# Both ends of a mixture-of-experts stage: where two engines' loops begin, extra identity transposes, and the first gathers' indices

## The chip, the cores and the metric

One core of a Trainium2 chip runs the whole program. The metric is device time in microseconds (us), the median of several executions. A profiled execution of its own gives the trace; its own time stands beside the span in the table below.

## What is computed

Input x has 8 sequences of 256 tokens with 512 features (2048 tokens, 16 tiles of 128), and a context of the same shape. The first half of the layer is grouped cross attention (32 query heads, 8 key and value heads). The second half, which the change touches, is a mixture of 32 experts with top 4 routing, each expert made of a large part (inner size 192) and a small shared part (inner size 128):

```python
x = x + xattn(layernorm(x), ctx, ctx, Wq, Wk, Wv, Wfc, bfc)
h = layernorm(x)
logits = h @ gate_w.T
rw = softmax(logits); _, sel = top_k(sigmoid(logits), 4)
w = take(rw, sel); w = w / w.sum(-1)
large = sum over e of (silu(h @ Wg[e]) * (h @ Wu[e]) * cw[e]) @ Wd[e]
small = the same with cWg, cWu, cWd, two experts sharing one chunk
x = x + large + 0.05 * small
```

All matrices are float32.

## The kernel before

There are three stages, each a block of its own with a program for every engine; all engines meet between two blocks.

**attention** (to about 396 us) computes the attention and stores the new x to `out` and its normalised rows to the table `xd` in device memory. ScalarE loads one set of function tables at its start (line 401) and uses the logarithm and the exponential there.

**route** (396 to 448 us) transposes the 16 tiles, computes the logits and the top 4, and sorts the (token, expert) pairs into slots of 128 rows, each slot of one expert. `transpose(t)` on TensorE (L1217) fills two PSUM buffers in turn; ScalarE's `x_evac(t)` (L1133) empties them, and transpose(t) waits for the evacuation of tile t - 2. ScalarE's program begins with `preload_act_table_set` (L1171), then two x_evac, then a logarithm and an exponential for the late tiles. Its results for the next stage are tables: `tok` (which rows of xd a slot gathers), `dst` (where its results are added), `slot_e`, `slot_buf`, and `turns` (how many loop turns there are). This input fills 78 slots. The weights of the first experts are loaded meanwhile.

**experts** (448 us to the end) runs the slots, two per loop turn; p is the slot's parity and selects one of two buffers. The loops are written for 48 turns with an `If(i < n)`, n = 39 here; the first turn (slots 0 and 1) stands ahead of the loop, and turns beyond n pass empty. For slot s:

- GpSimd `gather(s, p)`: waits until xg is free (turned and wt_ready of slot s - 2), copies column s of tok to gidx (L1501), waits for the copy, and gathers 128 rows of xd to xg with an indirect DMA (L1504).
- VectorE `turn(s, p)` (L1599): a 32 x 32 block transpose of xg into xb. `weights_of(s, p)` (L1590, L1592): the routing weights of the slot's expert. ScalarE `x_move(s, p)` (L1545): four transfers xb to xT, which finish the transpose.
- TensorE `gate_up(s)` (L1636): 8 matmuls for gates, 8 for ups. ScalarE `silu` (L1550). VectorE `gated(s)` (L1603, L1605): the product in `a`.
- TensorE `transpose_a(s)` (L1645): 3 transposes to at_ps, in the program of the next slot, ahead of its gate_up. VectorE `at_evac(s)` (L1582) copies them to aT. TensorE `down(s)` (L1653): 6 matmuls to y_ps, behind the next slot's gate_up.
- ScalarE `y_evac(s)` (L1556): y_ps to yb; it waits until the add of slot s - 2 has landed. GpSimd `add(s, p)`: copies column s of dst to yidx (L1510), waits for yb and until all earlier adds have landed (`y_added`), and adds yb to rows of `out` with an indirect DMA (L1518).

Each engine's order is written out by hand. VectorE's loop turn is at_evac(s - 1), turn(s + 2), gated(s), weights_of(s + 2), once for each parity; its last at_evac stands behind the loop. GpSimd's is add(s - 1), gather(s + 4), with the last add behind the loop. ScalarE's is silu(s), x_move(s + 2), y_evac(s - 1). TensorE's is transpose_a(s - 1), gate_up(s), down(s - 1), with transpose_a and down of the last slot behind the loop. Three weight buffers hold the experts; SyncE loads the next expert as slots finish.

Of the kernel before, what the change touches and what calls it, by code (L numbers as in the profile page):

```python
# [6 lines left out]
ACT = mybir.ActivationFunctionType  # L7
AX = mybir.AxisListType
F32 = mybir.dt.float32
# [5 lines left out]
P = 128  # L15
D = 512
# [950 lines left out]
IW = IL + IS  # L967
# [23 lines left out]
def route(nc, gw, gw_loaded, xs, ident, new, xd, out, tabs, wts, W, w_loaded, kept, xd_stored):  # L991
# [4 lines left out]
    tok, dst, slot_e, slot_buf, cum_i, turns = tabs  # L996
    with ExitStack() as ctx:  # L997
# [130 lines left out]
        def _(act):  # L1128
# [42 lines left out]
            act.preload_act_table_set("natural_log_exp_and_others")  # L1171
# [258 lines left out]
def experts(nc, ident, xd, out, tabs, wts, W, w_loaded):  # L1430
# [4 lines left out]
    with ExitStack() as ctx:  # L1435
# [10 lines left out]
        sg = [sb(f"sg{i}", [P, IW], F32) for i in range(2)]  # L1446
# [6 lines left out]
        at_ps, y_ps = ps("at_ps", [P, 4, P]), ps("y_ps", [P, D])  # L1453
# [41 lines left out]
        def _(pool):  # L1495
            def gather(s, p):

                if not (isinstance(s, int) and s < 2):
                    pool.wait_ge(turned, s - 1)
                    pool.wait_ge(wt_ready, s - 1)  # L1500
                pool.tensor_copy(idx[p][:, :], tok[:, bass.ds(s, 1)]).then_inc(idx_ready, 1)  # L1501
                pool.wait_ge(idx_ready, s + 1)
                pool.sem_inc(passed, 1)
                pool.indirect_dma_start(xg[p][:, :], None, xd[:, :], bass.IndirectOffsetOnAxis(idx[p][:, :], 0))\  # L1504
                    .then_inc(x_loaded[p], DMA)
# [17 lines left out]
            gather(4, 0)  # L1523
            add(0, 0)
            gather(5, 1)
            n, last = count(pool)
            with pool.Fori(1, NS // 2) as i:
                with pool.If(i < n):
                    for p in range(2):
                        add(i * 2 + p - 1, 1 - p)  # L1530
                        gather(i * 2 + p + 4, p)
# [6 lines left out]
        def _(act):  # L1538
# [24 lines left out]

            x_move(0, 0)
# [14 lines left out]
        def _(dve):  # L1579
# [40 lines left out]
            n, last = count(dve)  # L1620
            with dve.Fori(1, NS // 2) as i:  # L1621
                with dve.If(i < n):  # L1622
                    for p in range(2):
                        at_evac(i * 2 + p - 1, 1 - p)
                        turn(i * 2 + p + 2, p)
                        gated(i * 2 + p, p)
                        weights_of(i * 2 + p + 2, p)
            at_evac(last + 1, 1)

        @block.tensor  # L1630
        def _(pe):
            def gate_up(s, p, buf):
# [34 lines left out]

            slot(0, 0, first=True)
# [6 lines left out]
            transpose_a(last + 1, 1)  # L1675
            down(last + 1, 1, pe.value_load(slot_buf[0:1, bass.ds(last + 1, 1)], min_val=0, max_val=NW - 1))
# [63 lines left out]
```

## Time and profile before

| | |
|---|---|
| time, median of 3 runs | 1054.81 us (1053.97 to 1056.63) |
| profiled execution, its own time | 1054.6 us |
| its span, first to last instruction | 1052.9 us |
| mean granted TensorE clock (1.0 is 2.4 GHz, 0.5 is 1.2 GHz) | 0.968 |
| TensorE busy | 983.6 us, 93% |
| VectorE, ScalarE, GpSimd busy | 524.5, 314.0, 300.2 us |
| device memory | 101.29 MB read, 29.36 MB written |

Times within an execution count from the start of its span. PE is TensorE's matmuls, PEld its weight loads, DVE is VectorE, ACT ScalarE, POOL GpSimd, SP SyncE; a name with q, such as ACTq, is the engine's sequencer, which issues instructions and DMAs. A wait is put down to what released it; "issue" is time in which the engine waited for nothing that the profile shows. The profile shows the granted clock of TensorE for each stretch.

### The profile page before, as it was taken

The page shows a single profiled execution, that of the slowest core. Times are in us where ns is not written, and L with a number is a line of the kernel's source. Part 1 is how long each engine was busy: PE and PEld are TensorE (multiplying, and loading weights), DVE is VectorE, ACT ScalarE, POOL GpSimd, SP SyncE. Part 2 cuts the span into 40 slices and gives each one's busy share as a digit, 9 for nine tenths or more (in the row PEclk, how much of TensorE's full clock was granted, in tenths as well). Part 3 has the DMA queues.
Part 4 walks back from the last instruction along what each step waited for, and adds up shares of the span by engine and source line. Part 5 has one row for each costly group of instructions (what it writes and reads, how often), then busy time and mean ns, then how long its engine had stood idle before and what let it go on. Part 6 is the DMA issues. An engine that isn't in the chain of part 4 may idle for free.

```text
span 1052.9 us, 18703 instructions
## 1 busy us (share of the span) xinstructions
PE 983.6 (93%) x5163; PEld 723.9 (69%) x5164; DVE 524.5 (50%) x1233; ACT 314.0 (30%) x631; POOL 300.2 (29%) x399
## 2 busy tenths in 40 slices
PE   8789999999999987449999999999999999999994
PEld 6556667676665545337787777878777787877872
DVE  5677677777677727923333333333333333333331
ACT  2245465555555536801111111111111111111110
POOL 3012101011120002223443434344343443434432
PEclk9999999999999999569999999999999999999997
DMA  6153234331431019138888998989888899889563
GB/s 215 44 163 77 75 84 102 87 87 58 121 80 51 32 41 354 47 83 201 217 219 199 253 252 213 259 206 256 201 224 213 207 259 244 214 207 252 113 112 71
DMA packets 102603, 168.23 MB, mean 160 GB/s; under 512 B 15520, under 2 KB 65824, under 8 KB 98208
## 3 DMA queue, kind: packets, MB, share of 16 engines
q1 hardware_dynamic: 36624, 103.11, 31.3%
q0 software_dynamic: 17792, 43.30, 22.6%
q10 hardware_dynamic: 48144, 21.25, 7.3%
q8 instruction: 27, 0.44, 0.2%
q14 instruction: 16, 0.13, 0.0%
HBM read 101.29 MB, written 29.36 MB: 124 GB/s over the span
## 4 chain that ended last, share of the span: by engine, by line
PE 55%; DMA 1%; issue 1%; DVEq 0%; DVE 0%; ACTq 0%; POOL 0%; ACT 0%; POOLq 0%
PE y_ps L1653 19%; PE g_ps L1636 17%; PE u_ps L1636 16%; PE at_ps L1645 2%; DMA xg<-xd,gidx 0%; DMA xT<-xb 0%; ACTq L1545 0%; POOL out_x L1518 0%; DVEq L1621 0%; DVE xb L1599 0%; ACT sg L1550 0%; DVEq L1586 0%; ACT yb L1556 0%; DVE aT L1582 0%; DVEq L1622 0%
## 5 line engine op out<-in xcount | busy, mean ns | idle before, releaser
L1653 PE MATMUL y_ps<-W,aT 128*128 x468 | 216.2, 598 | 3.6 <-DVE aT L1582 3.6
L1518 POOL DMA_INDIRECT out_x<-yb,yidx x78 | 125.3, 1606 | 278.4 <-ACT yb L1556 159.7
L1636 PE MATMUL g_ps<-W,xT 128*128 x624 | 192.5, 452 | 12.8 <-DMA xT<-xb 12.8
L519 DVE TENSOR_REDUCE mx<-s 128x2 f32<-128x512 f32 x256 | 163.6, 682 | 59.4 <-PE s L710 58.6
L398 ACT ACTIVATE pt<-stp 128x512 f32<-128x512 f32 x256 | 139.1, 596 | 146.6 <-PE stp L724 145.9
L1636 PE MATMUL u_ps<-W,xT 128*128 x624 | 180.7, 432 | 0.0
L1636 PEld LDWEIGHTS g_ps<-W,xT 128*128 128x128 f32 x624 | 168.3, 311 | 15.2 <-issue 15.1
L1636 PEld LDWEIGHTS u_ps<-W,xT 128*128 128x128 f32 x624 | 171.0, 308 | 0.1
L1653 PEld LDWEIGHTS y_ps<-W,aT 128*128 128x128 f32 x468 | 89.6, 192 | 85.7 <-issue 79.6
L1599 DVE STREAM_TRANSPOSE xb<-xg 128x512 f32<-128x512 f32 x80 | 89.1, 1114 | 102.6 <-DMA xg<-xd,gidx 99.8
L1550 ACT ACTIVATE sg<-g_ps 128x320 f32<-128x320 f32 x78 | 34.2, 438 | 302.4 <-PE u_ps L1636 302.4
L1603 DVE SCALAR_TENSOR_TENSOR a<-u_ps,wt,sg 128x192 f32<-128x192 f32 x78 | 32.6, 418 | 160.8 <-ACT sg L1550 158.9
L1556 ACT COPY yb<-y_ps 128x512 f32<-128x512 f32 x78 | 45.7, 585 | 201.2 <-DMA out_x<-yb,yidx 125.4
L1504 POOL DMA_INDIRECT xg<-xd,gidx x82 | 82.7, 1008 | 65.4 <-POOL gidx L1501 64.7
L710 PE MATMUL s<-kst,qst 96*128 96x256 bf16 x512 | 81.6, 274 | 10.8 <-DVE mx L519 9.9
L1582 DVE COPY aT<-at_ps 128x384 f32<-128x384 f32 x78 | 43.5, 558 | 86.8 <-PE at_ps L1645 81.9
L724 PE MATMUL stp<-qst,kst 98*128 98x256 bf16 x512 | 78.5, 276 | 4.2 <-DMA qst<-nm 4.1
L710 PEld LDWEIGHTS s<-kst,qst 96*128 96x128 bf16 x512 | 43.7, 97 | 51.8 <-DVE mx L519 24.5
L740 PE MATMUL ov<-pt,vx 128*32 128x256 f32 x1024 | 70.3, 393 | 2.0 <-ACT xo L382 2.0
L1501 POOL COPY gidx<-tok 128x1 uint32 (+1 forms) x82 | 60.0, 732 | 28.1 <-POOLq L997 17.2
L724 PEld LDWEIGHTS stp<-qst,kst 98*128 98x128 bf16 x512 | 49.4, 98 | 17.7 <-issue 5.7
L1645 PEld LDWEIGHTS at_ps<-ident,a 128*128 128x128 f32 x234 | 30.2, 140 | 43.7 <-issue 42.0
(203 smaller groups left out, 869.5 us busy)
## 6 DMA issues: line engine op xcount, KB each, us to landing
W<-in_wts SPq DMA_DIRECT2D x32, 1280.0 KB
W<-in_wts SPq DMA_DIRECT2D x32, 768.0 KB
xT<-xb ACTq DMA_DIRECT2D x320, 64.0 KB
qst<-q SPq DMA_DIRECT2D x42, 256.0 KB, 5.0
xs<-in_x SPq DMA_DIRECT2D x8, 512.0 KB, 3.7
ctxT<-in_ctx SPq DMA_DIRECT2D x8, 512.0 KB, 4.2
out_x<-xs SPq DMA_DIRECT2D x16, 256.0 KB, 2.3
kst<-k SPq DMA_DIRECT2D x48, 64.0 KB, 2.3
```

Of the source, the lines that this page charges most:

```text
L398: act.activation(pt[g % 2][:, 2 * (j % 2) + r, :, :], stp[n % STP][:, :, :], ACT.Exp, scale=DH ** -0.5).then_inc(exp_done, 1)
L519: dve.tensor_reduce(mx[j // CH % 2][:, h:2 * G:G], s1[r][:, :, :], AX.X, ALU.max)\
L710: m = pe.matmul(s1[r][:, t, :], qst[b % 2][0:ROWS_QK, head(j, r), t * P:(t + 1) * P], kst[b % 2][0:ROWS_QK, head(j, r) // C, :], start=Tru ...
L724: m = pe.matmul(stp[n % STP][:, t, :], kst[b % 2][0:ROWS_ST, head(j, r) // C, t * P:(t + 1) * P], qst[b % 2][0:ROWS_ST, head(j, r), :], st ...
L740: m = pe.matmul(ov[c * VW:(c + 1) * VW, g % 2, :], vx[b % 2][:, t, g % 2 * C + c, :], pt[(b * G + g) % 2][:, c, t, :], start=(t == 0), sto ...
L1501: pool.tensor_copy(idx[p][:, :], tok[:, bass.ds(s, 1)]).then_inc(idx_ready, 1)
L1504: pool.indirect_dma_start(xg[p][:, :], None, xd[:, :], bass.IndirectOffsetOnAxis(idx[p][:, :], 0))\
L1518: pool.indirect_dma_start(out[:, :], bass.IndirectOffsetOnAxis(yidx[p][:, :], 0), yb[p][:, :], None, compute_op=ALU.add).then_inc(y_added, ...
L1599: dve.transpose(xb[p][:, :].rearrange("p (j r c) -> p j c r", r=Q, c=C), xg[p][:, 0:D]).then_inc(turned, 1)
L1636: m = pe.matmul(ps_[p][:, 0:IW], xT[p][:, :, c], W[:, bass.ds(buf, 1), (2 * c + g) * IW:(2 * c + g + 1) * IW] .rearrange("p a f -> p (a f) ...
L1645: m = pe.transpose(at_ps[:, c, :], a[p][:, c * P:(c + 1) * P], ident[:, :])
L1653: m = pe.matmul(y_ps[:, :], aT[p][:, c, :], W[:, bass.ds(buf, 1), GW + c * D:GW + (c + 1) * D].rearrange("p a d -> p (a d)"), start=(c == ...
```

## The change

In `route`, the explicit table load at the head of ScalarE's program goes. In `experts`:

- ScalarE begins with a Silu of one column of the identity, whose result nobody reads. It brings the table load of Silu to the start of its program.
- GpSimd's first four gathers take their indices from `tok` itself, with no copy and no wait for it; the others copy as before. gather(5) moves ahead of add(0), and the loop turn becomes gather(s + 4), add(s - 1).
- VectorE's at_evac(1) moves ahead of the loop, and a loop turn becomes turn(s + 2), gated(s), weights_of(s + 2), at_evac(s), for each parity. Nothing stands behind the loop.
- TensorE transposes the identity 32 times into a PSUM buffer of its own ahead of slot 0, and 5 times between the last transpose_a and the last down.

```diff
--- before.py
+++ after.py
@@ -1168,7 +1168,6 @@
                     act.activation(rown[:, t, :, :], away[t % 2][:, :, :], ACT.Relu, bias=number[:, t:t + 1],
                                    scale=minus[:, t:t + 1]).then_inc(rown_ready, 1)
 
-            act.preload_act_table_set("natural_log_exp_and_others")
             x_evac(0)
             x_evac(1)
             act.wait_ge(var_ready, 1)
@@ -1443,14 +1442,14 @@
         wt = [sb(f"wt{i}", [P, 2], F32) for i in range(2)]
         xb = [sb(f"xb{i}", [P, D], F32) for i in range(2)]
         xT = [sb(f"xT{i}", [P, P, C], F32) for i in range(2)]
-        sg = [sb(f"sg{i}", [P, IW], F32) for i in range(2)]
+        sg, first = [sb(f"sg{i}", [P, IW], F32) for i in range(2)], sb("e_first", [P, 1], F32)
         a = [sb(f"a{i}", [P, IP], F32) for i in range(2)]
         aT = [sb(f"aT{i}", [P, 3, P], F32) for i in range(2)]
         yb = [sb(f"yb{i}", [P, D], F32) for i in range(2)]
 
         g_ps = [ps(f"g_ps{i}", [P, 512]) for i in range(2)]
         u_ps = [ps(f"u_ps{i}", [P, 512]) for i in range(2)]
-        at_ps, y_ps = ps("at_ps", [P, 4, P]), ps("y_ps", [P, D])
+        at_ps, y_ps, idle_ps = ps("at_ps", [P, 4, P]), ps("y_ps", [P, D]), ps("idle_ps", [P, P])
 
         experts_ready, slots_done = sem("experts_ready"), sem("slots_done")
         idx_ready, x_loaded = sem("idx_ready"), [sem(f"xg_loaded{i}") for i in range(2)]
@@ -1498,10 +1497,14 @@
                 if not (isinstance(s, int) and s < 2):
                     pool.wait_ge(turned, s - 1)
                     pool.wait_ge(wt_ready, s - 1)
-                pool.tensor_copy(idx[p][:, :], tok[:, bass.ds(s, 1)]).then_inc(idx_ready, 1)
-                pool.wait_ge(idx_ready, s + 1)
-                pool.sem_inc(passed, 1)
-                pool.indirect_dma_start(xg[p][:, :], None, xd[:, :], bass.IndirectOffsetOnAxis(idx[p][:, :], 0))\
+                if isinstance(s, int) and s < 4:
+                    rows = tok[:, s:s + 1]
+                else:
+                    pool.tensor_copy(idx[p][:, :], tok[:, bass.ds(s, 1)]).then_inc(idx_ready, 1)
+                    pool.wait_ge(idx_ready, s - 3)
+                    pool.sem_inc(passed, 1)
+                    rows = idx[p][:, :]
+                pool.indirect_dma_start(xg[p][:, :], None, xd[:, :], bass.IndirectOffsetOnAxis(rows, 0))\
                     .then_inc(x_loaded[p], DMA)
 
             def add(s, p):
@@ -1521,14 +1524,14 @@
             for s in range(4):
                 gather(s, s % 2)
             gather(4, 0)
+            gather(5, 1)
             add(0, 0)
-            gather(5, 1)
             n, last = count(pool)
             with pool.Fori(1, NS // 2) as i:
                 with pool.If(i < n):
                     for p in range(2):
+                        gather(i * 2 + p + 4, p)
                         add(i * 2 + p - 1, 1 - p)
-                        gather(i * 2 + p + 4, p)
             add(last + 1, 1)
             pool.wait_ge(y_added, last * DMA + 2 * DMA)
             for p in range(2):
@@ -1561,6 +1564,7 @@
                 if not first:
                     y_evac(s - 1, 1 - p)
 
+            act.activation(first[:, :], ident[:, 0:1], ACT.Silu).then_inc(passed, 1)
             x_move(0, 0)
             x_move(1, 1)
             slot(0, 0, first=True)
@@ -1617,18 +1621,23 @@
             turn(3, 1)
             gated(1, 1)
             weights_of(3, 1)
-            n, last = count(dve)
+            at_evac(1, 1)
+            n, _ = count(dve)
             with dve.Fori(1, NS // 2) as i:
                 with dve.If(i < n):
                     for p in range(2):
-                        at_evac(i * 2 + p - 1, 1 - p)
                         turn(i * 2 + p + 2, p)
                         gated(i * 2 + p, p)
                         weights_of(i * 2 + p + 2, p)
-            at_evac(last + 1, 1)
+                        at_evac(i * 2 + p, p)
 
         @block.tensor
         def _(pe):
+            def keep_clock(n):
+
+                for _ in range(n):
+                    pe.transpose(idle_ps[:, :], ident[:, :], ident[:, :])
+
             def gate_up(s, p, buf):
                 pe.wait_ge(x_ready[p], moved(s, p))
                 for ps_, g in ((g_ps, 0), (u_ps, 1)):
@@ -1665,6 +1674,7 @@
                 if not first:
                     down(s - 1, 1 - p, pe.value_load(slot_buf[0:1, bass.ds(s - 1, 1)], min_val=0, max_val=NW - 1))
 
+            keep_clock(32)
             slot(0, 0, first=True)
             slot(1, 1)
             n, last = count(pe)
@@ -1673,6 +1683,7 @@
                     slot(i * 2, 0)
                     slot(i * 2 + 1, 1)
             transpose_a(last + 1, 1)
+            keep_clock(5)
             down(last + 1, 1, pe.value_load(slot_buf[0:1, bass.ds(last + 1, 1)], min_val=0, max_val=NW - 1))
 
 
```

## Rows read from the trace of the kernel before

**Rows 1.** The page: busy us (share of span) xinstructions of each engine

```profile
PE 983.6 (93%) x5163; PEld 723.9 (69%) x5164; DVE 524.5 (50%) x1233; ACT 314.0 (30%) x631; POOL 300.2 (29%) x399
```

**Rows 2.** Busy time by stretch: stretch, length, engines' busy, granted clock, DMA share, GB/s

```profile
480.00:1000.00 520.00, 519.95 (x1771) 408.21 (x1770) 188.58 (x426) 72.34 (x142) 212.76 (x284) 1.00 0.88 222
```

**Rows 3.** Timeline, routing stage's start: start, us, engine, what [idle before <- releaser]

```profile
396.26 1.28 ACT L1171 ACT_TABLE_LOAD   x1 [8.01 <-PEq L50]
...
396.30 1.06 PE L1217 MATMUL r_xt<-ident,xs 128*128 128x128 f32 x8 [1.85 <-PEq L50]
...
397.56 1.07 ACT L1133 COPY r_xnT<-r_xt 128x512 f32<-128x512 f32 x2
...
398.20 3.56 PE L1217 MATMUL r_xt<-ident,xs 128*128 128x128 f32 x16 [0.83 <-ACT r_xnT L1133]
```

**Rows 4.** Busy time by stretch, around three changes of the granted clock

```profile
398.00:399.00 1.00, 0.80 (x5) 0.77 (x6) 0.00 (x0) 0.97 (x4) 0.42 (x4) 0.76 0.77 236
463.00:464.00 1.00, 1.00 (x4) 0.86 (x3) 0.00 (x0) 0.00 (x0) 0.00 (x0) 0.81 0.00 0
1038.00:1040.00 2.00, 1.60 (x2) 0.84 (x3) 0.25 (x1) 0.00 (x0) 0.63 (x1) 0.50 0.70 135
```

**Rows 5.** Chain that ended last, expert stage's start: start, us, what

```profile
448.68 0.19 POOL gidx L1501
...
448.91 0.85 issue
449.77 3.58 DMA xg<-xd,gidx
...
459.66 4.25 PE g_ps L1636 x8
```

**Rows 6.** Timeline, the last 25 us

```profile
1030.44 2.74 PE L1653 MATMUL y_ps<-W,aT 128*128 x6
...
1032.47 0.15 DVE L1590 COPY wt<-xg 128x1 f32 x1 [0.68 <-DVE a L1605]
...
1033.43 0.58 ACT L1556 COPY yb<-y_ps 128x512 f32<-128x512 f32 x1 [2.36 <-DMA out_x<-yb,yidx]
...
1034.26 0.54 PE L1645 MATMUL at_ps<-ident,a 128*128 128x128 f32 x3 [1.08 <-issue]
1035.02 1.61 POOL L1518 DMA_INDIRECT out_x<-yb,yidx  x1 [2.60 <-ACT yb L1556]
...
1037.62 1.01 POOL L1504 DMA_INDIRECT xg<-xd,gidx  x1 [0.80 <-POOL gidx L1501]
1037.69 0.56 DVE L1582 COPY aT<-at_ps 128x384 f32<-128x384 f32 x1 [4.88 <-issue]
...
1038.40 5.43 PE L1653 MATMUL y_ps<-W,aT 128*128 x6 [3.60 <-DVE aT L1582]
...
1041.67 0.18 POOL L1510 COPY yidx<-dst 128x1 uint32 x1 [3.05 <-issue]
...
1043.95 0.58 ACT L1556 COPY yb<-y_ps 128x512 f32<-128x512 f32 x1 [9.93 <-PE y_ps L1653]
1045.54 1.61 POOL L1518 DMA_INDIRECT out_x<-yb,yidx  x1 [3.68 <-ACT yb L1556]
```

**Rows 7.** Timeline, expert stage's start: a gather and ScalarE's table load

```profile
457.66 0.98 POOL L1504 DMA_INDIRECT xg<-xd,gidx  x1 [0.79 <-issue]
...
459.79 1.28 ACT L1550 ACT_TABLE_LOAD   x1 [15.41 <-issue]
```

**Rows 8.** Tile out_x, adds' start to landing: first 480 to 1030 us, then from 1000

```profile
DMA to landing us min/median/max: 4.7/5.1/8.1
...
DMA to landing us min/median/max: 4.4/4.8/5.0
```

**Rows 9.** Chain that ended last, the eight up matmuls of a middle slot

```profile
484.81 2.15 PE u_ps L1636 x8
```

**Rows 10.** Timeline of GpSimd: an add that waited for the one before, and the next

```profile
632.61 1.60 POOL L1518 DMA_INDIRECT out_x<-yb,yidx  x1 [5.11 <-DMA out_x<-yb,yidx]
638.40 1.61 POOL L1518 DMA_INDIRECT out_x<-yb,yidx  x1 [1.99 <-ACT yb L1556]
```

## The prediction

> **What bounds the kernel now.** I read the page first, then the busy time by stretch, then the chain of waits at both ends of the expert stage, then the timeline there. The page has TensorE busy for 93% of the span [rows 1]. In the middle of the expert stage, from 480 to 1000 us, TensorE is busy 519.95 of 520 us at the full granted clock, while VectorE needs 188.58 us and GpSimd 212.76 us [rows 2]. Nothing in this stretch gives time back unless TensorE's own work shrinks, and the change leaves that work alone. A gain can only come from where TensorE waits: the start of the routing stage, the 13 us between the routing stage and the first expert matmul, and the last 20 us. I cost the change place by place, against the profiled execution's 1054.6 us (its span is 1052.9 us), which lies 0.2 us under the median of 1054.81 us.
>
> **Part 1, the table load in the routing stage.** ScalarE begins the stage with a load of 1.28 us at 396.26, and its first copy of a transposed tile follows at 397.56 [rows 3]. TensorE has begun its first eight transposes at 396.30; the first four, which the copy needs, take about half of their 1.06 us plus the tail of one, so they end near 396.93. TensorE resumes only at 398.20, after that copy [rows 3]. Without the load the copy starts near 396.96: 397.56 - 396.96 = 0.6 us earlier. The stage up to its tables is a chain of TensorE, ScalarE and VectorE with no outside date in it that I found, so 0.6 us carries through. Bounds: 0 (if the function tables must be loaded before the logarithm after all, see the rivals) and 1.28 + 0.3 us (if the earlier transposes also keep the clock up; it falls at 398 to 399 after 1.1 us of transposes and a gap [rows 4]). I take 0.6, since the row shows which transposes the copy must still await. The Trainium skill ("ScalarE: Activation LUTs", What ACT_TABLE_LOAD costs) adds a drain of about 1.38 us to the 1.28 us of a load, and by it the removal could be worth up to 2 us; here the copy follows 0.02 us after the load, so the trace does not agree.
>
> **Part 2, the first gathers.** The chain runs index copy 448.68 (0.19 us), 0.85 us without any wait, gather 449.77, which lands 3.58 us later; then the transpose, four transfers to xT, and the first expert matmul at 459.66 [rows 5]. The copy and its semaphore go: 0.19 + about 0.1 us. Whether the 0.85 us goes too depends on whose it is. In the last 20 us the same 0.80 us stands ahead of a gather at 1037.62, and 1.01 us stands between the end of yb at 1044.53 and the last add at 1045.54, where no copy lies in between [rows 6]. So a DMA_INDIRECT starts 0.8 us after its release whatever released it, and I let the 0.85 us stay: gain 0.3 us, bounds 0.2 and 1.1. The Trainium skill ("DMA: Bandwidth & Descriptors", Latency and other measured facts) gives about 1 us as the first-byte latency of a DMA issued by GpSimd, which speaks for the gap being the DMA's own and against this edit. Against the gain: gather 1 can follow gather 0 at once instead of waiting a second for its own copy, and gather 3 comes 1.2 us before its 457.66 [rows 7], so its data moves beside the first xT transfers. An add lands 4.4 to 5.0 us after its start in the last 50 us and 5.1 in the middle, with weight loads beside it [rows 8], so company costs some 0.5 to 1 us; only a part of it can meet xT(0). I take -0.15, which leaves 0.15 us; with both ends -0.6 to +1.1.
>
> **Part 3, the table load of Silu** moves from 459.79 to the stage's start. Both places are hidden: it ends at 461.07 [rows 7] while the activation waits until 466.1 for the matmuls, and at the start ScalarE waits until 454.49 for the first transpose. Nothing, unless the start shrinks by 4 us.
>
> **Part 4, 32 transposes before slot 0.** TensorE is free from 447 to 459.66. Sixteen transposes take 3.56 us at a mostly low clock, small gaps included [rows 3], 0.22 us each, so 32 take about 7.1 us from 448.7 and end by 455.8, or by 457.4 at 0.27 us each, before the first matmul near 459.4: no delay. Do they help? The first slot's 16 matmuls take 459.66 to 466.08, 6.42 us, and the clock rises inside, in 463 to 464 [rows 4]; at the full clock eight of them take 2.15 us [rows 9], sixteen 4.3 to 4.4, so 2.0 us is there to win. But once the clock has risen the rest of the 32 goes by fast, and TensorE idles for 2 to 5 us before slot 0. At the routing stage's start it had 1.85 us idle, 1.1 us of transposes, a gap, and fell to half [rows 4]. I take 0 for the forecast, bounds -0.6 (the clock rises later relative to an earlier start) and +2.0. The Trainium skill ("TensorE: Matmul & The Clock Gate", What's actually happening) says the window is free-running and does not reset with the kernel, so the point of the rise differs between runs; no row of one execution can show that.
>
> **Part 5, the loops in the middle.** VectorE's cyclic order (at_evac, turn, gated, weights_of) is unchanged. GpSimd's becomes gather(s+4) before add(s-1). The gather waits for weights_of, which ends 2 us after slot s's up matmuls (the last one at 1032.62); the add waits for yb, which ends 1.4 us later (1034.01) [rows 6]. So the gather runs first without holding the add for long: copy 0.2, gap 0.8, gather 1.0, copy 0.2, gap 0.85, so the add starts about 0.7 us later in each slot than now. ScalarE needs that add landed two slots (14.66 us) later. An add lands 5.1 us after its start, 8.1 at worst [rows 8], so 3 us of slack stay: nothing.
>
> **Part 6, the end.** Step by step from [rows 6]:
> - VectorE now finishes weights_of at 1032.81, then passes nine empty turns of its loop (39 of 48 are used) and reaches the last at_evac only at 1037.69, though the transposes were done at 1034.80. Inside the loop at_evac starts at 1034.85, ends 1035.41, and TensorE starts down 0.14 us later, at 1035.55 instead of 1038.40: 2.85 us.
> - The five transposes begin at 1034.80 and take 5 x 0.11 to 0.16 us at the full clock (three take 0.54 with their tail), so they end at about 1035.5: free. Down now runs at half clock, 5.43 us [rows 4, 6], where the slot before took 2.74 us. The stretch 1038 to 1040 is at half, behind an idle from 1034.80 to 1038.40, so with TensorE busy I expect 2.74: another 2.7 us. Down ends near 1038.3 instead of 1043.83.
> - ScalarE's last yb comes after its own empty turns. It dispatches the yb before at 1033.43; nine turns at VectorE's 0.53 us give 1038.2, a tie. It ends at 1038.95 instead of 1044.53, 5.6 us earlier.
> - GpSimd is late next. gather(81) now comes first: released at 1032.62, started near 1033.65, over at 1034.66; copy, gap, and add(76) starts at 1035.7 instead of 1035.02. Its empty turns end near 1039.7 (now the gather at 1037.62 is dispatched 0.7 us earlier, and the next copy is at 1041.67: 4.7 us). But the last add must await the landing of add(76), and this add now has a gather 2 us ahead of it. A landing takes 4.4 to 5.0 us in the last 50 us [rows 8]; with company up to 1 us more. I take 5.5: landed at 1041.2, plus 0.8, last add at 1042.0 instead of 1045.54. Gain 3.5 us; bounds 2.9 (landing 6.1) and 5.6 (landing hidden, the ScalarE date). What follows the last add is unchanged.
>
> **Sum.** 0.6 + 0.15 + 3.5 = 4.25 us off 1054.6: 1050.35, and with the 0.2 us to the median 1050.5 us. Its own range, with landing and gather bounds: 1049.2 to 1051.9.
>
> **Rivals.**
> - The clock survives into slot 0. For: there are 32 transposes, and a run of them keeps TensorE busier than anything since 420 us. Against: the idle behind them. It gives 2.0 us more: 1048.5.
> - The last add is not held by the landing of the one before, so the whole 5.6 us comes through. For: an early landing, of 4.4, and a GpSimd order that yields faster than I reckon. Against: five adds in a row at 4.8 to 5.0. It gives 2.1 us more: 1048.4.
> - The change does not do what it says in the routing stage: with no explicit load, one is put before the logarithm anyway. Nothing is saved, or one more load of 1.28 us is paid between logarithm and exponential. With the first gathers disturbing xT as well (-0.6), the sum is 0 - 0.6 + 3.5 = 2.9 or less: 1051.9. Against: the attention stage uses logarithm and exponential with a single load, and the trace shows no load between.
> - Slower: adds queue behind gathers. Each add awaits the one before, so adds are spaced at least landing + 0.8 us; a slot is 7.33 us, and it decides from a mean landing of 6.5 us. The median is 5.1, and a gather 2 us ahead may add up to 1 us and more under the weight loads (8.1 is in the record [rows 8]). At 7.0 the surplus is 0.47 us in each of 76 slots, 36 us less the 5 us that the double buffers hold: 1054.8 - 4 + 31 = 1082. Adds that await the one before sit idle for up to 5.11 us where the usual is 3.5, and the next is back in step [rows 10], which speaks against.
>
> **Chances.** Forecast 0.52, clock in slot 0 0.17, landing hidden 0.10, load put back or start disturbed 0.15, slower 0.06. A measurement of this kernel tells 0.3%, 3.2 us, from no change: faster means under 1051.65. The first three cases lie there but for 0.04 of the forecast's own: 0.75. Same: 0.15 + 0.04 = 0.19. Slower: 0.06. The range holds 8 in 10 from 1047.9 (part of both faster rivals) to 1052.3.
>
> **What would show it.** Right: no ScalarE load in the routing stage and its first copy about 0.7 us after its start; the first GpSimd gather 0.8 us after the stage opens; the first expert matmul still in a stretch of half clock; at_evac within 0.1 us of the last transposes; down in 2.7 us; the last add released by the landing of the add before it. Wrong: a stretch inside 480 to 1000 us with TensorE idle, a landing over 6.5 us in the middle, or the last add released by yb.

## The result and the profile after

The changed kernel took 1047.54 us (median of 5, 1046.58 to 1049.79) against 1054.2 us for the kernel before in the same comparison: a ratio of 0.9938, 95% interval 0.9915 to 0.996. Two later comparisons, each on one chip, gave 0.9948 (0.993 to 0.9967) and 0.9949 (0.9926 to 0.9972). So it saves 5.4 to 6.7 us, 0.5 to 0.6%. The forecast was 1050.5 us, a saving of 4.3, and its range began at 1047.9: the sign was right, the size too small. The measured median lies 0.4 us below the range; the medians of the two later comparisons, 1048.3 and 1048.23 us, lie inside it, so that it lies outside at all is partly chance.

The profiled execution took 1049.79 us, its span 1048.1. The page of the changed kernel has TensorE with more work, the 37 added transposes, in a shorter span (busy us, share of the span, instructions), and TensorE's wait for xT, ahead of its gates, at 4.4 us where 12.8 stood, since the transposes fill the rest (group of instructions: busy us, mean ns, idle before and its releaser):

```profile
PE 988.3 (94%) x5200; PEld 730.1 (70%) x5201; DVE 522.7 (50%) x1233; ACT 312.6 (30%) x631; POOL 297.8 (28%) x395
...
L1645 PE MATMUL g_ps<-W,xT 128*128 x624 | 192.4, 451 | 4.4 <-DMA xT<-xb 4.4
```

I cut both profiled executions at the same events, read from the timelines, in us:

| stretch | before | after | difference | forecast |
|---|---|---|---|---|
| attention: span's start to the first transpose of the routing stage | 396.30 | 397.52 | +1.22 | 0 |
| routing stage, to its last table | 51.84 | 50.12 | -1.72 | -0.6 |
| last table to gather 0 | 1.63 | 1.30 | -0.33 | -0.3 |
| gather 0 to the first expert matmul | 9.89 | 10.22 | +0.33 | +0.15 |
| slot 0: first matmul to its silu | 6.44 | 7.17 | +0.73 | 0 |
| silu to the first transposes of a | 1.20 | 1.21 | +0.01 | 0 |
| slots: first to last transposes of a | 566.96 | 565.75 | -1.21 | 0 |
| end: last transposes of a to the span's end | 18.64 | 14.81 | -3.83 | -3.5 |
| span | 1052.9 | 1048.1 | -4.8 | -4.25 |

The pair differs by 4.8 us, the medians by 6.7. The attention stage, whose code is the same, ends between 394.01 and 399.10 us in the sixteen executions profiled for this study, so a single time carries up to 5 us that no edit made. From here on I compare stretches.

**Routing stage.** Timeline of the changed kernel, against [rows 3]. The load is gone and nothing took its place. The copy starts 0.66 us behind the first transpose instead of 1.26, TensorE idles 0.24 instead of 0.83 us, and its next transposes come at full speed:

```profile
397.52 1.06 PE L1216 MATMUL r_xt<-ident,xs 128*128 128x128 f32 x8 [1.85 <-PEq L50]
...
398.18 1.07 ACT L1133 COPY r_xnT<-r_xt 128x512 f32<-128x512 f32 x2 [8.71 <-PE r_xt L1216]
...
398.82 1.15 PE L1216 MATMUL r_xt<-ident,xs 128*128 128x128 f32 x8 [0.24 <-ACT r_xnT L1133]
```

**Start of the expert stage.** Chain that ended last (start, us, what), against [rows 5]. The 0.19 us of the index copy are gone and the wait without a name stays: 0.90 us, where 0.85 stood:

```profile
448.04 0.90 issue
448.94 3.57 DMA xg<-xd,tok
```

**First slot.** Timeline and busy time by stretch. The 32 transposes take 6.57 us; the clock rises near their end, at 454.1, and falls again at 457.5, 1.6 us before the first matmul. It is back in 464 to 465 only, later into the slot than in [rows 4]:

```profile
448.19 6.57 PE L1639 MATMUL idle_ps<-ident 128*128 128x128 f32 x32 [1.80 <-PEq L997]
...
459.16 4.65 PE L1645 MATMUL g_ps<-W,xT 128*128 x8 [4.40 <-DMA xT<-xb]
```

```profile
457.00:458.00 1.00, 0.00 (x0) 0.00 (x0) 0.00 (x0) 0.00 (x0) 0.00 (x0) 0.77 0.73 261
464.00:465.00 1.00, 1.00 (x4) 0.81 (x3) 0.00 (x0) 0.00 (x0) 0.00 (x0) 0.82 0.00 0
480.00:1000.00 520.00, 520.00 (x1775) 409.38 (x1774) 185.74 (x426) 72.58 (x142) 212.02 (x284) 1.00 0.85 223
```

**The end.** Timeline, against [rows 6]. VectorE's copy comes 0.04 us behind the transposes' end, down starts at 1034.59 and takes 2.84 us instead of 5.43:

```profile
1033.29 0.54 PE L1654 MATMUL at_ps<-ident,a 128*128 128x128 f32 x3 [1.10 <-issue]
...
1033.67 0.71 PE L1639 MATMUL idle_ps<-ident 128*128 128x128 f32 x5
1033.87 0.56 DVE L1586 COPY aT<-at_ps 128x384 f32<-128x384 f32 x1 [2.50 <-PE at_ps L1654]
1034.59 2.84 PE L1662 MATMUL y_ps<-W,aT 128*128 x6 [0.20 <-DVE aT L1586]
1034.75 1.60 POOL L1521 DMA_INDIRECT out_x<-yb,yidx  x1 [1.14 <-DMA out_x<-yb,yidx]
1037.54 0.59 ACT L1559 COPY yb<-y_ps 128x512 f32<-128x512 f32 x1 [4.48 <-PE y_ps L1662]
...
1040.35 1.59 POOL L1521 DMA_INDIRECT out_x<-yb,yidx  x1 [1.37 <-DMA out_x<-yb,yidx]
```

The chain of its last 20 us shows what is late next. Two adds wait one for the other, and each landing (4.88 and 4.76 us) stands in the chain:

```profile
1029.04 4.88 DMA out_x<-yb,yidx
...
1034.75 4.76 DMA out_x<-yb,yidx
...
1040.35 1.59 POOL out_x L1521
```

The last yb is ready at 1038.13; the last add waits until 1039.51 for the landing and starts 0.84 us later.

### The profile page after: what moved, and what is told of

It is laid out like the page before. It is cut to its first block, busy times and chain, and to the rows that moved or that the text cites. A ratio compares the mean times of both kernels' runs of the same rounds, so it can differ in the third digit from the quotient of the medians.

```text
span 1048.1 us, 18692 instructions
## 1 busy us (share of the span) xinstructions
PE 988.3 (94%) x5200; PEld 730.1 (70%) x5201; DVE 522.7 (50%) x1233; ACT 312.6 (30%) x631; POOL 297.8 (28%) x395
## 4 chain that ended last, share of the span: by engine, by line
PE 54%; DMA 2%; issue 1%; POOL 0%; DVE 0%; ACTq 0%; ACT 0%; DVEq 0%; POOLq 0%
PE y_ps L1662 18%; PE g_ps L1645 17%; PE u_ps L1645 16%; PE at_ps L1654 2%; DMA out_x<-yb,yidx 1%; DMA xg<-xd,tok 0%; DMA xT<-xb 0%; ACTq L1548 0%; POOL out_x L1521 0%; DVE xb L1603 0%; POOL xg L1507 0%; ACT sg L1553 0%; DVEq L1590 0%; DVE a L1607 0%; DVE a L1609 0%
## 5 line engine op out<-in xcount | busy, mean ns | idle before, releaser
L1662 PE MATMUL y_ps<-W,aT 128*128 x468 | 213.7, 592 | 0.2 <-DVE aT L1586 0.2
L1507 POOL DMA_INDIRECT xg<-xd,gidx x78 | 78.5, 1007 | 64.4 <-POOL gidx L1503 62.2
L1503 POOL COPY gidx<-tok 128x1 uint32 (+1 forms) x78 | 14.3, 183 | 196.4 <-DVE wt L1594 196.4
```

The lines of the kernel that those rows point to most:

```text
L1662: m = pe.matmul(y_ps[:, :], aT[p][:, c, :], W[:, bass.ds(buf, 1), GW + c * D:GW + (c + 1) * D].rearrange("p a d -> p (a d)"), start=(c == ...
```

## The experiments

My theory was that the terms of the sum are the right ones and that the surplus over the forecast is the clock's, which rises and falls at other places in each execution. The rival was that the changed kernel differs in something fixed, such as the middle of the stage, to which the forecast gave nothing. Kernels are named by their labels. All stretches of all traces stand in one table behind the runs.

**The changed kernel once more, `after_again`.** 

> The changed kernel once more, for a second trace. My theory: of the 6.7 us between the medians, 4.8 us stand in the profiled pair, and the rest is where TensorE's clock rises and falls, which differs between executions; so this trace shows the clock changes of routing stage and first slot at other places, a routing stage of 50 to 52.5 us and a first slot of 4.5 to 7.2 us, and the same last 15 us within 0.3 us. Rival: the changed kernel differs from the old one in something fixed that the first pair hid (then routing stage and first slot are as in the first trace within 0.2 us). Both: ratio near 0.994, 1047 to 1049 us.

1048.3 us, ratio 0.9948. Routing stage 50.12, slots 565.77, end 14.89 us: each within 0.1 us of the first trace. The gather to the first matmul took 11.28 instead of 10.22 us. So the shorter routing stage and the shorter middle are fixed, and the rival is right on these two, where the theory failed; the start of the stage is what varies.

**VectorE's part alone, `at_evac_in_loop`.** The kernel before with

```diff
             weights_of(3, 1)
+            at_evac(1, 1)
...
-                        at_evac(i * 2 + p - 1, 1 - p)
                         turn(i * 2 + p + 2, p)
                         gated(i * 2 + p, p)
                         weights_of(i * 2 + p + 2, p)
-            at_evac(last + 1, 1)
+                        at_evac(i * 2 + p, p)
```

> The kernel before with VectorE's part alone: at_evac at the end of the loop turn. My theory: the last at_evac follows the last transposes within 0.1 us and down starts 2.9 us earlier, but GpSimd's old order now ends last: its index copy for the last add comes only after gather 81 and nine empty loop turns, at about 18.6 - 11.2 = 7.4 us behind the last transposes as before, so the last add starts 8.2 to 8.4 us behind them instead of 11.28: 3.0 us less. Without the five transposes down takes between 2.7 and 4.5 us, which is hidden. Median 3 us below before. Rival (the landing of the add before is what holds the last add): it starts 35.02 + 4.9 + 0.8 - 34.26 = 6.5 us behind the transposes, 4.8 us less.

Ratio 0.9988 (0.9972 to 1.0004). Its timeline:

```profile
1034.14 0.54 PE L1645 MATMUL at_ps<-ident,a 128*128 128x128 f32 x3 [1.12 <-issue]
1034.72 0.56 DVE L1582 COPY aT<-at_ps 128x384 f32<-128x384 f32 x1 [2.08 <-PE at_ps L1645]
1034.89 1.61 POOL L1518 DMA_INDIRECT out_x<-yb,yidx  x1 [2.63 <-ACT yb L1556]
1035.44 2.84 PE L1653 MATMUL y_ps<-W,aT 128*128 x6 [0.75 <-DVE aT L1582]
```

at_evac follows at once, down takes 2.84 us without any added transposes, and the last add starts 8.69 us behind the last transposes instead of 11.28: close to the 8.2 to 8.4 of GpSimd's old order and its empty turns, far from the 6.5 of the landing. The end is 16.26 instead of 18.64 us. By the ratio that makes 1.3 us in all, where 3 were expected. But the slots took 568.35 us, 1.4 us more than in the kernel before, and TensorE was busy for only 518.48 us of the 520 in the middle. The waits of TensorE in that stretch (us in total, times, longest) name the transfers to xT, which the prediction had left out:

```profile
PE g_ps L1636 <- DMA xT<-xb: 1.4, 2, 1.2
```

**GpSimd's part alone, `gather_first`.** The kernel before with

```diff
-            add(0, 0)
             gather(5, 1)
+            add(0, 0)
...
-                        add(i * 2 + p - 1, 1 - p)
                         gather(i * 2 + p + 4, p)
+                        add(i * 2 + p - 1, 1 - p)
```

> The kernel before with GpSimd's part alone: gather 5 ahead of add 0, and gather ahead of add in the loop turn. My theory as predicted: nothing in the middle, nothing at the end (the last add still waits for yb), 0 us. Rival, from the comparison of the two traces: before has six slots that are 0.2 to 0.3 us longer than 7.33 us, the changed kernel none, and this order removes them: the time from the first transposes of a to the last is 565.7 us instead of 567.0, 1.2 us less.

Ratio 0.9977 (0.9959 to 0.9996), 2.4 us less. The slots took 565.75 us, as in the changed kernel: the rival is right and the forecast's "nothing" wrong. Its routing stage, with the load in place, took 50.70 us; the clock did not fall in it.

**The load of the routing stage alone, `after_no_preload_only`.** The kernel before without the line `act.preload_act_table_set(...)` in `route`. 

> The kernel before without the explicit table load in the routing stage, nothing else. My theory: no other load takes its place; ScalarE's first copy starts 0.66 us after the first transpose instead of 1.26; TensorE's idle behind its first eight transposes falls from 0.83 to 0.24 us, and with it the clock stays at full through the first 5 us; the stage, from first transpose to the tables, takes 50.1 us instead of 51.84 (clock fell) or 50.70 (it did not). Rival (the shorter stage of the changed kernel was only the clock's chance): 51.2 us, 0.6 less than 51.84, with the clock down at 398 to 402. Medians: 1 to 1.7 us below before, or 0.6.

The routing stage took 50.10 us, the clock stayed at full, and no other load appeared. The ratio was 1.0008 (0.9988 to 1.0027): an edit that shortens its stage by 0.6 to 1.7 us in the traces can't be seen in the time at all, so this one is shown by the trace only.

**Small gathers, `before_small_gathers`.** The kernel before, with

```diff
-                pool.indirect_dma_start(xg[p][:, :], None, xd[:, :], bass.IndirectOffsetOnAxis(idx[p][:, :], 0))\
+                n, rows = (XW, xd[:, :]) if isinstance(s, int) else (68, xd.rearrange("n (k w) -> (n k) w", w=68))
+                pool.indirect_dma_start(xg[p][:, 0:n], None, rows, bass.IndirectOffsetOnAxis(idx[p][:, :], 0))\
```

> The kernel before, with its order on GpSimd, but each gather from slot 6 on brings only 68 columns instead of 544 (as many rows and descriptors, an eighth of the bytes; the rest of its tile keeps old values, so this leaves the experts' inputs out). My theory: the long slots in the middle (2 to 6 per execution, 1.1 to 2.6 us together) are slots in which the transfers to xT run beside the gather, which the old order starts 0.5 us ahead of them, and beside a weight load, and land late; with small gathers no slot is long, and first to last transposes take 565.77 us as with the new order. Rival (the new order helps by starting adds or gathers earlier, not by moving the gather's bytes away from xT's): 566.9 to 568.4 us as before.

The slots took 565.74 us with GpSimd's old order, and of the distances between the transposes of one slot and the next none was long but those that all these kernels have, the first (7.41 us) and the last (8.58 us, with the empty turns in it). So it is the gathers' bytes. Ratio 0.9987 (0.9973 to 1.0001): the time does not tell it from the kernel before, the stretches do. The timelines of one slot show where they were: in the kernel before the gather starts 0.5 us ahead of the four transfers to xT, and its data move beside them,

```profile
1015.61 1.01 POOL L1504 DMA_INDIRECT xg<-xd,gidx  x1 [0.80 <-POOL gidx L1501]
...
1016.11 2.52 ACTq L1545 DMA_DIRECT2D xT<-xb  x4
```

and in the changed kernel it starts 3.2 us behind them:

```profile
1015.13 2.60 ACTq L1548 DMA_DIRECT2D xT<-xb  x4
...
1018.34 1.01 POOL L1507 DMA_INDIRECT xg<-xd,gidx  x1 [0.80 <-POOL gidx L1503]
```

Sometimes xT then comes too late for the next slot. All seventeen long slots in the four traces with the old order and full gathers follow 7.0 to 7.1 us behind the issue of a weight load; but so do some 190 of the 283 slots there that are not long. That a weight load is needed is therefore likely, and what else picks the late ones is not shown. This is the longest case, in the chain of at_evac_in_loop, a slot of 8.81 us (the weight load began at 884.67):

```profile
884.49 8.63 DMA xT<-xb
893.12 0.24 issue
893.36 2.54 PE g_ps L1636 x8
```

**No empty turns, `before_39_turns`.** The kernel before with `Fori(1, 39)` for `Fori(1, NS // 2)` in the four loops. 

> The kernel before with the four loops written for 39 turns, as many as this input needs, instead of 48, so no empty turn is passed (the output is right for this input alone). My theory: the nine empty turns are what held the last at_evac (3.43 us behind the last transposes), delayed the last transposes on TensorE (1.08 us idle before them) and GpSimd's last copy. Here at_evac follows within 0.6 us of the transposes' start with VectorE's old order, the slot before them is 1.1 us shorter, down takes 2.7 to 2.8 us, and from the last transposes to the end 13.8 to 14.5 us pass instead of 17.5 to 18.6: together 4.5 to 5.5 us. Rival (at_evac was late for another reason on VectorE, such as the wait for its own weights_of): it stays 3 us behind.

1047.41 us, ratio 0.9933 (0.9911 to 0.9956): as much as the whole change. Its first to last transposes take 565.36 us: the last slot is 7.3 us long instead of 8.6, and three slots with late xT remain. The timeline has at_evac at once and no 1.1 us of idle before the last transposes:

```profile
1031.21 0.49 PE L1645 MATMUL at_ps<-ident,a 128*128 128x128 f32 x3
...
1031.74 0.56 DVE L1582 COPY aT<-at_ps 128x384 f32<-128x384 f32 x1 [0.73 <-PE at_ps L1645]
1032.50 2.84 PE L1653 MATMUL y_ps<-W,aT 128*128 x6 [0.81 <-DVE aT L1582]
```

The end took 15.29 us, more than the 13.8 to 14.5 expected: here too the last add waits for the landing of the one before, which starts 2.03 us behind the last transposes.

**Without the five transposes, `after_no_5`.** 

> The changed kernel without the five transposes between the last transpose_a and the last down. My theory: they are free and they give nothing either. Down starts 1.30 us behind the last transposes with or without them, since VectorE's copy ends then; without them down takes 2.84 us, or up to 4.5 if the clock falls; the last add waits for the landing of the add before it, at 7.1 to 7.3 us behind the last transposes, where yb is ready at 4.84; so the end stays at 14.8 to 14.9 us unless down takes more than 5.2 us. Rival (they hold the clock for down, and down decides): the end is 1.6 to 2.7 us later.

Down takes 2.84 us and starts 1.29 us behind the last transposes, the end 14.91 us, median 1048.32; ratio 0.996 (0.9943 to 0.9976). The five do nothing.

```profile
1032.47 0.56 DVE L1586 COPY aT<-at_ps 128x384 f32<-128x384 f32 x1 [2.51 <-PE at_ps L1654]
1033.18 2.84 PE L1662 MATMUL y_ps<-W,aT 128*128 x6 [0.75 <-DVE aT L1586]
```

**Without the 32, `after_no_32`.** 

> The changed kernel without the 32 transposes ahead of slot 0. My theory: they neither help nor harm, since TensorE idles 2.5 to 7 us behind them and the clock falls before or early in slot 0: slot 0 takes 6.3 to 7.5 us with or without, the gather to the first matmul 10.2 to 11.3 us as with them (its cost is the gathers'). Median within 1 us of the changed kernel, 1047.5 to 1048.5. Rival (the transposes' reads disturb the transfers): the gather to matmul time falls to 9.9 us with them gone.

Slot 0 took 7.22 us, the gather to the first matmul 10.14. The median was 1049.77 us (8 runs, 1045.13 to 1051.48), above the 1047.5 to 1048.5 expected, but the ratio, 0.9944 (0.9924 to 0.9963), is that of the changed kernel. The 32 do nothing either.

**72 of them, `after_72`.** 

> The changed kernel with 72 transposes before slot 0 instead of 32, so that TensorE is busy from the stage's opening to near the first expert matmul. My theory: 32 end at 454.8 and the clock falls again at 457.5, before slot 0, so they give nothing; 72 (about 27 at half clock, 0.2 us each, then 45 at 0.11 us: 10.3 us) end at about 458.5, the clock stays up, and slot 0's 16 matmuls take 4.4 to 4.7 us instead of 6.4 to 7.2: 2 to 2.7 us below the changed kernel. If the clock rises late they run on to at most 460, 1 us past the start of slot 0. Rival (transposes of the identity hold no clock through slot 0, or delay it): 0 or 1 us more than the changed kernel.

They took 9.6 us instead of 10.3, since the clock rose after 3 us, and ended 2.45 us before the first matmul. It fell again at 458.4, 1.4 us into slot 0, which took 6.42 us. The expectation failed; its number of transposes was too small. 1046.5 us, ratio 0.993 (0.9911 to 0.9949): 1.8 us under after_again on the same chip, which the stretches behind the attention stage do not explain (their sum is 0.4 us smaller), so nothing shows it to be a gain of the 72.

**Copies for gathers 1 to 3, `after_copies_1_to_3`.** The changed kernel with

```diff
-                if isinstance(s, int) and s < 4:
+                if isinstance(s, int) and s < 1:
...
-                    pool.wait_ge(idx_ready, s - 3)
+                    pool.wait_ge(idx_ready, s)
```

> The changed kernel, but only gather 0 takes its indices from tok; gathers 1 to 3 copy them first, as before. My theory: the time from gather 0's start to the first expert matmul was 9.89, 9.89 and 9.95 us in three kernels whose gathers 1 to 3 copy, and 10.22, 11.28 and 11.29 us in three whose gathers don't, so the earlier gathers run beside the transfers to xT(0) and cost 0.3 to 1.4 us, more than the 0.33 us that the missing copy of gather 0 gives. Here that time is 9.9 us, and the opening of the stage to gather 0 stays at 1.30 us from the tables: about 0.3 to 1.4 us less than the changed kernel up to slot 0. Rival (the longer time is something else, such as the 32 transposes or the early table load of Silu beside the transfers): it stays at 10.2 to 11.3 us.

10.05 us from the gather to the first matmul where 9.9 were expected, against 10.13 to 11.29 with the direct gathers in six traces. The median, 1048.37, does not show it.

**96 transposes and two gathers fewer, `best_96_skip`.** 

> The changed kernel with three edits: 96 transposes ahead of slot 0 instead of 32, only gather 0 straight from tok, and the last two gathers, whose rows no slot uses, left out. My theory: with 72 transposes TensorE was still idle for 2.45 us before slot 0 and the clock fell 1.7 us into it; 24 more at 0.11 us fill this, so slot 0 takes 4.5 us instead of 6.4 to 7.2 (unless the clock rises late: then they run up to 2 us into slot 0). Gather 0 to the first matmul 9.9 us instead of 10.2 to 11.3. At the end the add before the last starts 0.75 us behind the last transposes instead of 1.5, with no gather beside it, and lands after 4.4 us instead of 4.8: last add at 5.9 to 6.2 us instead of 7.1 to 7.3. Together 2 + 0.8 + 1.1 = 3.9 us below the changed kernel, near 1044 us. Rival (the end is held by GpSimd's nine empty turns and its index copy): last add at 6.8 us or later; and if the transposes delay slot 0, 1 us more there.

The transposes took 12.48 us and ran 1.4 us past the arrival of xT (VectorE's third block transpose, which waits for the same transfers, started at 457.09, the first matmul at 458.59). Slot 0 took 4.72 us. From gather 0 to the silu of slot 0 16.33 us passed, against 17.39 to 18.11 in the changed kernel, 16.33 in after_copies_1_to_3 and 14.98 and 15.09 with 80 transposes (below), so the delay took much of the gain back. At the end the add before the last started 1.62 us behind the last transposes although no gather stood ahead of it, 1.9 us after its yb was ready at 1030.01; I don't know why it took this long. The median, 1048.89 us, is no better than the changed kernel's, where 1044 was expected.

**80 transposes and the copies, `after_80_copies`.** The changed kernel with the edit of after_copies_1_to_3 and `keep_clock(80)`. 

> The changed kernel with 80 transposes instead of 32 and copies for gathers 1 to 3. 96 overran the arrival of xT by 1.4 us at an early rise of the clock (12.5 us in all), 72 ended 2.45 us short at 9.6. My theory: 80 take 10.5 us, up to 11.7 where the clock rises late, and xT arrives about 11.2 us after TensorE's start, so the clock stays up and slot 0 takes 4.5 to 4.7 us, at a gather to matmul of 9.9 to 10.4: 2 to 2.5 us less than the changed kernel up to the first transposes of a. Median 1046 to 1046.5. Rival (free-running changes of the clock take it away in part of the executions, and the overrun in others, so on the median nothing is left): 1048.

Timeline: 80 take 10.26 us, TensorE idles 0.75 us, the clock stays at full, and the eight gates take 2.54 us instead of 4.65:

```profile
447.57 10.26 PE L1639 MATMUL idle_ps<-ident 128*128 128x128 f32 x80 [1.80 <-PEq L997]
...
458.58 2.54 PE L1645 MATMUL g_ps<-W,xT 128*128 x8 [0.75 <-DMA xT<-xb]
```

Slot 0 took 4.73 us. 1047.04 us, ratio 0.9928 (0.9907 to 0.9949), where 1046 to 1046.5 was expected.

**The two side by side, `after_third` and `after_80_third`.** 

> The changed kernel, beside after_80_third on one chip. My theory: routing stage 50.1 us, slots 565.77 us, last 14.6 to 14.9 us as in both traces before; gather to first matmul 10.2 to 11.3, slot 0 6.3 to 7.5, attention anywhere from 394 to 399 us. 1047.5 to 1048.5 us.

> The kernel with 80 transposes and copies for gathers 1 to 3, beside the changed kernel on one chip. My theory: slot 0 at 4.7 us, the gather to the first matmul 9.9 to 10.3 us, everything else equal, so 2.3 us below after_third on the median, and spread as wide, since the spread is the attention stage's. Rival: the difference is lost where the clock rises late, and the two medians are within 1 us.

On one chip 1048.23 us (11 runs, 1046.11 to 1053.7; ratio 0.9949) and 1045.2 us (6 runs, 1044.14 to 1048.06; ratio 0.9924, 0.9894 to 0.9955): 3.0 us less. The intervals of the two ratios overlap, so the traces carry this more than the times: 4.73 us for slot 0 in both traces of the kernel with 80, 6.8 to 7.7 us in the three of the changed kernel. This is the lowest ratio of the study, though its interval overlaps with several others.

All stretches, in us:

| kernel | routing | gather 0 to matmul | slot 0 | slots | end |
|---|---|---|---|---|---|
| before | 51.84 | 9.89 | 6.44 | 566.96 | 18.64 |
| at_evac_in_loop | 51.85 | 9.89 | 6.37 | 568.35 | 16.26 |
| gather_first | 50.70 | 9.95 | 7.49 | 565.75 | 17.93 |
| after_no_preload_only | 50.10 | 9.95 | 7.40 | 566.89 | 17.47 |
| before_39_turns | 50.71 | 9.96 | 7.45 | 565.36 | 15.29 |
| before_small_gathers | 50.73 | 9.89 | 7.41 | 565.74 | 18.19 |
| changed kernel, three traces | 50.12, 50.12, 50.10 | 10.22, 11.28, 10.13 | 7.17, 6.83, 7.69 | 565.75, 565.77, 565.78 | 14.81, 14.89, 14.63 |
| after_no_5 | 50.11 | 10.36 | 7.26 | 565.78 | 14.91 |
| after_no_32 | 50.11 | 10.14 | 7.22 | 565.77 | 14.56 |
| after_72 | 50.13 | 11.29 | 6.42 | 565.76 | 14.92 |
| after_copies_1_to_3 | 50.12 | 10.05 | 6.28 | 565.77 | 14.55 |
| best_96_skip | 50.10 | 11.61 | 4.72 | 565.77 | 14.72 |
| after_80_copies, two traces | 50.12, 50.10 | 10.25, 10.36 | 4.73, 4.73 | 565.77, 565.73 | 14.82, 14.85 |

## Why the prediction was right and wrong

**What bounds the kernel: half right.** Most of the gain lies at the ends, but not all of it. The prediction read 519.95 busy of 520 us [rows 2] as "nothing here gives time back". Some waiting does not show there: in the kernel before five slots were 0.17 to 0.31 us longer than 7.33, their eight gates took 2.45 to 2.54 us in the chain instead of 2.27, and this counted as busy. A list of the distances between the transposes of a would have shown them.

**Part 1, table load: mechanism right, size at the lower of its bounds.** 0.6 us for the load is exact (1.26 to 0.66 us, and 50.70 to 50.10 where the clock stayed up in both). With the load it fell in two of five traces and cost 1.1 us (51.84 against 50.70); without the load it fell in none of eleven. So few traces don't show that the load brings the fall, only that it goes with it. The mean of the term is 51.2 - 50.1 = 1.1 us.

**Part 2, first gathers: the gain right, the loss too small.** The wait of 0.85 us did not go with the copy, as taken; the copy gave 0.33 us. The rule behind it, 0.8 us "whatever released it", is too wide: in the changed kernel gather 1, which waits for nothing, starts 0.30 us behind the end of gather 0. The Trainium skill ("DMA: Bandwidth & Descriptors", Latency and other measured facts) gives about 1 us as the first-byte latency of a DMA issued by GpSimd; that is another stretch than the wait ahead of the gather, and doesn't explain it. In both traces the DMA engines moved nothing for 1.8 us behind the start of gather 0, so they don't agree with 1 us counted from there.

Gather 0 to the first matmul took 9.89 to 9.96 us in the six traces of old kernels and 10.13 to 11.29 in the six with direct gathers; most of the difference is in the last of the four transfers to xT(0), which landed after 2.92 us in the kernel before and after 3.07 to 4.32 us in these. Against 0.33 us of gain that is a small loss for the start. It isn't shown to be the gathers' alone: with the copies restored it was still 10.05 to 10.36 in three traces of kernels with transposes and an early load of Silu (one more, with 96 transposes, was held by these), and without the 32 transposes 10.14. The early load of Silu was not tested by itself; what disturbs the transfers stays open.

**Part 3** was right as far as shown: the load of Silu ends at 449.43, before ScalarE's first transfer at 453.68. Whether it costs something in the transfers is the open point of part 2.

**Part 4, the 32 transposes: right,** nothing (6.3 to 7.7 us with, 7.2 without). The rival "the clock survives into slot 0" had about the right price, 2.0 us, and too few transposes for it: with 80 slot 0 takes 4.73 us.

**Part 5, the loops in the middle: wrong, and this is the step that failed.** The prediction asked what the new order does to the adds and found slack, which is right: no add held anything, and the slower rival did not come. It did not ask what each DMA runs beside once its start moves by 3.7 us. So it put the middle at nothing, where 1.21 us went in the pair and 1.6 us on the mean of the traces: the gather left the transfers to xT, and 1.1 to 2.6 us of late xT went (566.9 to 568.35 us against 565.75 to 565.78). Two runs show it from both sides: the new order alone (565.75), and the old order with an eighth of the gathers' bytes (565.74). The second term that was too small is the clock in part 1.

**Part 6, the end: right.** -3.5 forecast, -3.83 in the pair, 2.6 to 4.1 over all traces, since down at a falling clock takes 4.24 to 5.43 us in the old kernels. at_evac, down at 2.84 us, the five transposes free, the add before the last at 1.44 us behind the transposes (1.46 measured) and the last add held by its landing all came as reckoned. The landing took 4.8 us where 5.5 was taken, so the last add came 4.2 us earlier behind the transposes and not 3.5. That the end is still near -3.5 is partly luck: what follows the last add took 0.4 us more in this trace (it varies by as much between traces), where the prediction had it unchanged. A detail was missed: the add before the last is itself held by the landing of the one before it, not by the gather. No run has VectorE's and GpSimd's parts alone together; that the end needs both is read from their single runs (16.26 and 17.93 us) and the 14.55 to 14.92 us of the kernels with both.

**The sum.** 1.1 + 0.3 - 0.8 + 0 + 1.6 + 3.3 = 5.5 us from the means of the table, against 5.4, 6.2 and 6.7 us in three comparisons. The forecast lacked 0.5 us of the clock in the routing stage and 1.6 us of the middle, and had 0.65 us too much at the start (the -0.8 is 0.65 for the gather to the first matmul and 0.15 for slot 0). The range was too narrow below. Its own lower end, 1049.2 us, doesn't follow from its bounds: 0.6 for the load, 1.1 for the start and 4.6 for the end with the earliest landing of 4.4 us give 1048.5, and with the 1.6 us bound of the load 1047.5. And a median of five carries about 1 us of the attention stage's spread, by my estimate from the sixteen traces.

## What to carry to other kernels

- When the order of DMA-issuing steps changes, list for each transfer what it will run beside, before and after. A transfer with slack that moves away from one without slack is a gain that the table of busy time did not show here.
- Work behind a loop with spare turns waits until the sequencer has passed them all: nine empty turns cost this kernel as much as the whole change brought. Put the last step inside the turn, and then look at the engine whose last step is still outside.
- Keeping TensorE busy pays only if the work reaches up to the matmuls that are to be fast. Here too little (32, 72) gave nothing, and too much (96) was paid back in part as a delay.

## What was not expected of the hardware

- Nine empty turns of a loop take 4.8 us on VectorE, 0.53 us each.
- A redundant table load of 1.28 us costs 0.6 us by itself. In two of five traces that had it the clock fell behind it, which cost 1.1 us more; it fell in none of the eleven without.
- The first indirect DMA of the stage starts 0.90 us behind the stage's opening although its indices are ready and it waits for nothing else; the next one, which waits for nothing either, starts 0.30 us behind the end of the first.
- TensorE's clock fell to half 2.8 to 5.2 us after the 32 transposes had ended, in each of five traces, with nothing between; 80 transposes with 0.4 to 0.75 us of idle behind them held it through the first slot.
